# Scattering the second half's rows to the experts: a copied, looped form against a written-out form paced by TensorE's tiles

## The chip, the cores and the metric

One core of a Trainium2 chip runs the whole program. The metric is the device time of that core in microseconds (us), smaller is better. The kernel is written by hand: every engine (PE = TensorE, DVE = VectorE, ACT = ScalarE, POOL = GpSimd, SP = SyncE) has its own instruction list, and semaphores order them.

## What is computed

The reference, cut to what matters here. 64 batches of 128 tokens with 128 features pass four layers:

```python
x = x + tanh(g_xattn[0]) * _L0_xattn_ref(_layernorm(x), ctx_1024, ...)   # attention over 77 context rows
x = x + tanh(g_ffn[0])   * _L0_ffn_ref(_layernorm(x), Wg, bg, bias, W1, b1, W2, b2)
x = x + tanh(g_xattn[1]) * _L1_xattn_ref(_layernorm(x), ctx_1024, ...)
x = x + tanh(g_ffn[1])   * _L1_ffn_ref(_layernorm(x), kernel, ...)

def _L0_ffn_ref(x, Wg, bg, bias, W1, b1, W2, b2):      # mixture of 16 experts, the best 2 for each token
    logits = einsum('sbd,de->sbe', x, Wg) + bg + bias
    vals, idx = top_k(logits, 2)
    w = softmax(vals - max(vals)); cw = einsum('sbk,sbke->sbe', w, one_hot(idx, 16))
    h = relu(einsum('sbd,edh->esbh', x, W1) + b1)      # 128 -> 256
    y = einsum('esbh,ehd->esbd', h, W2) + b2           # 256 -> 128
    return einsum('esbd,sbe->sbd', y, cw)
```

The kernel computes each expert only for the tokens that chose it. For that the tokens' rows are sorted by expert through a buffer in DRAM.

## The kernel before

**Stages.** Stage A (0 to about 465 us in the trace) is the first attention layer and the expert choice, one batch per step. Stage B (about 480 to 704 us) is the experts. Stage C (from about 704 us) gathers each token's two results and does the second attention layer and the last layer.

**Halves.** The 64 batches are routed in two halves of CB = 32. When a half's logits are there, `route(c)` computes for each token two slot numbers, `POS[0]` and `POS[1]` (128 partitions x 64 batches, int32). Half 0 is routed in the middle of stage A (ROUTE0 = 40 steps), half 1 after the end of stage A. The expert input rows of all batches are kept in SBUF in `XN` (128 x 64 x 128, float32, written at L544).

**Scatters.** POOL writes each batch's 128 rows twice, once for each of the two chosen experts, to the DRAM buffer `xs_dram[c]` (the trace calls it moe_rows), with an indirect DMA of 64 KB each. The helper `scatter(c, b, p)`, L508 to L519, does one batch: it waits until the DMAs of two batches ago have landed (the semaphore `scat_made{p}`, p the parity, counts 16 for each DMA), copies the batch's row tile from `XN` to a small buffer `scat[p]` (L512), copies two columns of slot numbers to `si` (L514, two instructions), waits for these three copies (L515), and issues the two indirect DMAs (L518). Half 0's scatters lie between POOL's steps of stage A. Half 1's stand behind stage A on POOL, in a loop of 16 turns with two batches each, L564 to L566, with register addresses.

**Experts.** Each half has NT = 80 tiles of 128 rows, so stage B has 160 tiles. SP loads the tiles in groups of four (20 groups a half): `load_group`, L421 to L426, waits until TensorE has transposed all but one of the groups loaded before (`xsT_mm` counts tiles whose first transpose, L1318, is done), then issues a 256 KB load into one of two buffers `xsb`. `store_group`, L428 to L433, stores four finished tiles (L432), three groups behind the load. In front of the first load of each half, SP waits in `scattered(c)`, L415 to L419, for all 64 scatter DMAs of that half. SP's list is in order: load, store, load, store; while it waits in `scattered(1)` it stores nothing either. TensorE does per tile one transpose (L1318), one matrix product into 256 columns, two transposes (L1304) and two products, with tile t's parts spread over six steps so that the neighbours overlap. DVE adds the biases (L1053, L1046), ACT copies and applies relu (L656, L719).

**After the scatters** POOL waits for all of them to land, makes a few constants of stage C (L573 to L588), waits for half 0's stored results (L642) and issues the first gathers (L595), which read the slot numbers straight from `POS[k][:, b:b + 1]`.

The functions that the change touches:

Of the kernel before, what the change touches and what calls it, by code (L numbers as in the profile page):

```python
# [52 lines left out]
def wait_free(engine, sem, value):  # L53

    if isinstance(value, int) and value <= 0:
        return
    engine.wait_ge(sem, value)  # L57
# [31 lines left out]
def flamingo_two_layers(nc, a, out, xs_dram, ys_dram):  # L89
    NB, N, D = a["x"].shape  # L90
# [8 lines left out]
    CB = NB // NCH  # L99
# [27 lines left out]
    with ctx:  # L127
        def sb(name, shape, dt=F32):
            return ctx.enter_context(nc.sbuf_tensor(name, shape, dt))

        def sem(name):
            return ctx.enter_context(nc.semaphore(name))
# [3 lines left out]
        XN = sb("moe_in", [P, NB, D])  # L136
# [6 lines left out]
        POS = [sb(f"slot{k}", [P, NB], I32) for k in range(2)]  # L143
# [155 lines left out]
        s = {n: sem(n) for n in names}  # L299
# [3 lines left out]
        xs_flat = [xs_dram[c] for c in range(NCH)]  # L303
# [8 lines left out]
        def apart(engine):  # L312

            engine.nop(nofuse=True)  # L315
# [156 lines left out]
        def _(pool):  # L472
            g = nc.gpsimd
# [34 lines left out]
            def scatter(c, b, p):  # L508

                bb = b + c * CB  # L510
                wait_free(pool, s[f"scat_made{p}"], (bb - p) * 16)
                g.tensor_copy(scat[p], XN[:, bass.ds(bb, 1), :].rearrange("q o d -> q (o d)")).then_inc(s["idx_made"], 1)  # L512
                for k in range(2):
                    g.tensor_copy(si[2 * p + k], POS[k][:, bass.ds(bb, 1)]).then_inc(s["idx_made"], 1)  # L514
                pool.wait_ge(s["idx_made"], bb * 3 + 3)  # L515
                apart(pool)
                for k in range(2):
                    g.indirect_dma_start(out=xs_flat[c][:, :], out_offset=bass.IndirectOffsetOnAxis(ap=si[2 * p + k], axis=0),  # L518
                                         in_=scat[p], in_offset=None).then_inc(s[f"scat_made{p}"], 16)  # L519
# [41 lines left out]
            pool.wait_ge(s["ro_done"], 2)  # L561
            pool.wait_ge(s["xs_zeroed1"], 16 * CB)
            pool.wait_ge(s["XN_kept"], NB)
            with pool.Fori(0, CB // 2) as turn:  # L564
                for p in range(2):
                    scatter(1, turn * 2 + p, p)  # L566

            pool.wait_ge(s["w1_loaded"], 16 * len(loads1))
            pool.wait_ge(s["kq_step"], SETUP_STEPS)
# [4 lines left out]
            for q in range(GH):  # L574
# [3 lines left out]
                                in_=one_hot[strip, :].rearrange("q (h k) -> q h k", h=GH), compare_op=ALU.not_equal, fill=1.0,  # L578
                                base=0, pattern=[[-1, GH], [0, KW]], channel_multiplier=1).then_inc(s["c_consts"], 1)
                pool.wait_ge(s["c_consts"], 4 + 5 * q + 1)  # L580
                for c in range(NKB):
                    h, k = divmod(GH * c + q, NKB)
# [870 lines left out]
```

## Time and profile before

| | us |
|---|---|
| three timed runs | 1169.97, 1174.06, 1175.59 |
| median | 1174.06 |
| the profiled execution | 1175.44 |
| its span, first to last instruction | 1173.7 |
| PE busy in the span | 1038.0 (88%) |
| DVE, ACT, POOL busy | 821.1, 586.3, 648.8 |

The page of the profile has the busy time of each engine, the span cut into 40 slices of 29.3 us, the DMA queues, the chain that ended last, and the costliest groups of instructions. In the timelines, a row is: start in us from the span's start, duration in us, engine, line and operation, output<-inputs, how many of them in sequence (xN), and in brackets how long the engine had been idle and what ended that. "SPq" is SP's queue, which issues the DMAs of loads and stores. "PEclk" is the granted clock of TensorE as a share of 2.4 GHz; 0.5 is 1.2 GHz.

### The profile page before, as it was taken

How to read it: one execution, taken by the hardware profiler on the slowest of the kernel's cores; microseconds unless marked ns; L12 is line 12 of the kernel's file. 1: busy time of each engine (PE TensorE's matmuls, PEld its weight loads, DVE VectorE, ACT ScalarE, POOL GpSimd, SP SyncE). 2: the span in 40 equal slices, each digit the busy share in tenths (PEclk: the TensorE clock that was granted, in tenths of full speed). 3: DMA queues.
4: the chain of work that ended last, by engine and by line, in shares of the span. 5: the costliest groups of instructions: out<-in, count | busy, mean ns of one | idle time of the engine just before them, and what ended most of it. 6: DMA issues, size and time to landing. Idle time of an engine off the chain costs nothing. (4 is left out here: it accounts for less than half of the span.)

```text
span 1173.7 us, 40437 instructions
## 1 busy us (share of the span) xinstructions
PE 1038.0 (88%) x13498; PEld 847.5 (72%) x13498; DVE 821.1 (70%) x2572; ACT 586.3 (50%) x1415; POOL 648.8 (55%) x1155
## 2 busy tenths in 40 slices
PE   4999999987999995699859996899999999998893
PEld 4788887865777774488758984677777777776672
DVE  1777777776777775655525555778888888887784
ACT  2666666653566662244425552345545545454464
POOL 2333333323777677567640005477777777777756
PEclk9999999997999997699979996999999999999997
DMA  3422113221443300244333331111111111111101
GB/s 74 88 49 46 38 45 75 72 68 45 106 105 89 90 19 29 84 137 145 107 92 112 109 91 48 32 30 37 44 40 43 44 40 43 43 41 41 39 24 31
DMA packets 106902, 74.39 MB, mean 63 GB/s; under 512 B 21360, under 2 KB 98288, under 8 KB 106736
## 3 DMA queue, kind: packets, MB, share of 16 engines
q1 hardware_dynamic: 98544, 55.40, 18.0%
q0 software_dynamic: 8192, 16.79, 4.7%
q8 instruction: 102, 1.67, 0.6%
q14 instruction: 64, 0.52, 0.2%
HBM read 38.60 MB, written 33.55 MB: 61 GB/s over the span
## 5 line engine op out<-in xcount | busy, mean ns | idle before, releaser
L656 ACT ACTIVATE arena<-PS 77x512 f32<-77x512 f32 (+4 forms) x736 | 304.9, 441 | 454.9 <-PE PS L1172 265.5
L1172 PE MATMUL PS<-arena 128*32 128x128 f32 (+5 forms) x9488 | 452.6, 291 | 49.9 <-issue 16.7
L1172 PEld LDWEIGHTS PS<-arena 128*32 128x32 f32 (+4 forms) x9488 | 352.0, 145 | 129.7 <-issue 37.1
L1172 PE MATMUL PS<-w,arena 128*128 x960 | 191.7, 318 | 1.2 <-ACT arena L656 0.4
L518 POOL DMA_INDIRECT moe_rows<-arena x128 | 127.4, 996 | 71.8 <-POOL arena L514 49.5
L533 POOL TENSOR_TENSOR arena<-arena,minus_half 128x2 f32<-128x2 f32 (+1 forms) x70 | 47.5, 679 | 188.3 <-DVE arena L830 166.6
L595 POOL DMA_INDIRECT arena<-moe_results,slot x128 | 128.7, 1005 | 40.7 <-issue 31.6
L1172 PEld LDWEIGHTS PS<-w,arena 128*128 128x128 f32 x960 | 135.5, 195 | 17.0 <-issue 4.5
L637 POOL TENSOR_TENSOR arena<-arena,minus_half 128x2 f32<-128x2 f32 (+1 forms) x71 | 51.1, 720 | 172.7 <-DVE arena L1151 168.9
L1053 DVE TENSOR_TENSOR arena<-PS,b_rows 128x256 f32<-128x256 f32 x160 | 67.8, 424 | 79.0 <-PE PS L1172 65.5
L1172 PEld LDWEIGHTS PS<-arena,wk_wq 128*128 128x128 f32 x512 | 80.6, 198 | 45.6 <-issue 43.0
L1172 PE MATMUL PS<-wo,arena 128*128 128x128 f32 x640 | 100.0, 288 | 2.2 <-ACT arena L656 1.4
L1172 PE MATMUL PS<-arena,wk_wq 128*128 128x154 f32 x512 | 98.3, 317 | 1.5 <-ACT arena L656 0.8
L1065 DVE TENSOR_REDUCE arena<-PS 128x8 f32<-128x616 f32 x128 | 96.0, 791 | 3.3 <-PE PS L1172 3.2
L719 ACT ACTIVATE arena<-PS 128x256 f32<-128x256 f32 x160 | 61.4, 384 | 72.7 <-PE PS L1304 66.9
L1172 PEld LDWEIGHTS PS<-wo,arena 128*128 128x128 f32 x640 | 83.9, 193 | 13.6 <-ACT arena L656 3.4
L744 ACT ACTIVATE arena<-PS 128x1536 f32<-128x1536 f32 x64 | 93.3, 1457 | 0.0
L540 POOL TENSOR_TENSOR arena<-arena 128x616 f32<-128x616 f32 x64 | 78.1, 1220 | 21.6 <-DVE arena L896 21.5
L867 DVE TENSOR_REDUCE arena<-PS 128x8 f32<-128x616 f32 x64 | 51.2, 800 | 54.2 <-PE PS L1172 54.2
L1046 DVE TENSOR_TENSOR arena<-PS,b_rows 128x128 f32<-128x128 f32 x160 | 46.1, 288 | 34.3 <-PE PS L1172 31.3
L1249 PE MATMUL PS<-ident,arena 128*77 128x128 f32 x512 | 68.8, 277 | 1.1 <-ACT arena L656 0.9
L1126 DVE RECIPROCAL arena<-PS 128x128 f32<-128x128 f32 x64 | 61.1, 954 | 12.3 <-PE PS L1172 8.8
(149 smaller groups left out, 1656.5 us busy)
## 6 DMA issues: line engine op xcount, KB each, us to landing
moe_rows<-zeros SPq DMA_DIRECT2D x64, 160.0 KB, 2.5
arena<-moe_rows SPq DMA_DIRECT2D x40, 256.0 KB
moe_results<-arena SPq DMA_DIRECT2D x40, 256.0 KB
residual<-in_x SPq DMA_DIRECT2D x64, 64.0 KB
w<-in_W SPq DMA_DIRECT2D x32, 128.0 KB
arena<-in_ctxC SPq DMA_DIRECT2D x64, 64.0 KB
out<-arena SPq DMA_DIRECT2D x64, 64.0 KB, 1.6
arena<-in_ctxT SPq DMA_DIRECT2D x32, 77.0 KB
```

What stands on the lines that cost most here:

```text
L518: g.indirect_dma_start(out=xs_flat[c][:, :], out_offset=bass.IndirectOffsetOnAxis(ap=si[2 * p + k], axis=0), in_=scat[p], in_offset=None). ...
L540: g.tensor_tensor(pv, pv, rd0[t.par(3)].rearrange("q (h o) -> q h o", o=1).to_broadcast([P, H0, J]), ALU.mult).then_inc(s["P0_made"], 1)
L595: g.indirect_dma_start(out=gy[k][p], out_offset=None, in_=ys_flat[c][:, :], in_offset=bass.IndirectOffsetOnAxis(ap=POS[k][:, b:b + 1], axi ...
L656: A.activation(o, i, ACT.Copy).then_inc(s[done], 1)
L719: A.activation(hT[p], PS[:, 4 + p, 0:EH], ACT.Relu).then_inc(s["hT_cp"], 1)
L744: A.activation(PT1[t.par(6)].rearrange("q (g w) -> q g w", g=NG), PS[:, 4:4 + NG, 0:TAIL], ACT.Exp, scale=DH1 ** -0.5).then_inc(s["exp1"], 1)
L867: V.tensor_reduce(mx0.rearrange("q (k h) -> q k h", k=2), sv, X, ALU.max).then_inc(s["mx0_made"], 1)
L1053: V.tensor_tensor(hb[p], PS[:, 2 + p, 0:EH], b1s[:, bass.ds(e, 1), :].rearrange("q o h -> q (o h)"), ALU.add).then_inc(s["h_made"], 1)
L1065: V.tensor_reduce(mx1[:, 2 * i * KEYS:2 * (i + 1) * KEYS].rearrange("q (g k) -> q g k", g=2)[:, :, 0:GH], PS[:, 2 * i:2 * i + 2, 0:GH * J] ...
L1126: V.reciprocal(rd1, PS[:, 1, 0:P]).then_inc(s["rd1_made"], 1)
L1172: return T.matmul(o, l, r, start=start, stop=stop)
L1249: last = T.transpose(PS[0:J, 2 + h // HB0, (h % HB0) * P:(h % HB0 + 1) * P], P0[p][:, h * J:(h + 1) * J], ident[:, :])
```

## The change

Half 1's loop over `scatter(1, ...)` is replaced by 32 batches written out at build time.

- The row tile isn't copied: the DMA's source is `XN[:, b, :]`.
- The slot numbers aren't copied: the DMA's index list is `POS[k][:, b:b + 1]`.
- The wait for the three copies is gone with them. The wait for the landing of the DMAs of two batches ago stands, with a constant.
- New: batch number n of the half (n = b - 32) waits until TensorE has transposed 2n tiles (`xsT_mm`), so batch 31 waits for 62 tiles of the 80 of half 0.

Half 0's scatters are left as they are.

```diff
             pool.wait_ge(s["XN_kept"], NB)
-            with pool.Fori(0, CB // 2) as turn:
-                for p in range(2):
-                    scatter(1, turn * 2 + p, p)
+            for b in range(CB, NB):
+
+                p = b % 2
+                pool.wait_ge(s[f"scat_made{p}"], (b - p) * 16)
+                wait_free(pool, s["xsT_mm"], 2 * (b - CB))
+                apart(pool)
+                for k in range(2):
+                    g.indirect_dma_start(out=xs_flat[1][:, :],
+                                         out_offset=bass.IndirectOffsetOnAxis(ap=POS[k][:, b:b + 1], axis=0),
+                                         in_=XN[:, b, :], in_offset=None).then_inc(s[f"scat_made{p}"], 16)
```

`apart` is an empty instruction that carries a wait of its own; `wait_free` leaves out a wait for zero or less.

## Rows read from the trace of the kernel before

**Rows 1.** The page: PE's busy tenths and granted clock in 40 slices.

```profile
PE   4999999987999995699859996899999999998893
PEclk9999999997999997699979996999999999999997
```

**Rows 2.** Waits of SP's DMA queue, 480 to 700 us: total, times, longest.

```profile
SPq L57 <- DMA moe_rows<-arena: 20.0, 1, 20.0
```

**Rows 3.** Timeline of SP around the change of halves.

```profile
573.00 0.38 SPq L425 DMA_DIRECT2D arena<-moe_rows  x1
575.45 0.39 SPq L432 DMA_DIRECT2D moe_results<-arena  x1
596.28 0.37 SPq L425 DMA_DIRECT2D arena<-moe_rows  x1
```

**Rows 4.** Timeline of POOL: half 1's first instruction, one batch's period, the end.

```profile
478.82 0.29 POOL L512 COPY arena<-moe_in 128x128 f32 x1 [5.41 <-DVE tile_experts L992]
...
587.75 0.30 POOL L512 COPY arena<-moe_in 128x128 f32 x1
587.99 0.30 POOL L514 COPY arena<-slot 128x1 int32 x2
589.07 0.98 POOL L518 DMA_INDIRECT moe_rows<-arena  x1 [0.78 <-POOL arena L514]
590.35 0.96 POOL L518 DMA_INDIRECT moe_rows<-arena  x1 [0.30 <-issue]
591.31 0.30 POOL L512 COPY arena<-moe_in 128x128 f32 x1
...
593.91 0.96 POOL L518 DMA_INDIRECT moe_rows<-arena  x1 [0.30 <-issue]
596.28 1.15 POOL L573 MEMSET arena<- 128x384 f32 x4 [1.42 <-DMA moe_rows<-arena]
```

**Rows 5.** Timeline of PE: last tile of half 0, first five of half 1.

```profile
582.56 0.27 PE L1318 MATMUL PS<-ident,arena 128*128 128x128 f32 x1
...
598.97 0.48 PE L1318 MATMUL PS<-ident,arena 128*128 128x128 f32 x1 [15.04 <-DMA arena<-moe_rows]
...
606.54 0.27 PE L1318 MATMUL PS<-ident,arena 128*128 128x128 f32 x1
```

**Rows 6.** Windows, L1318 on PE alone: stretch, length, busy (count), clock, DMA share, GB/s.

```profile
489.00:583.00 94.00, 20.17 (x74) 1.00 0.44 132
606.00:699.00 93.00, 20.71 (x76) 1.00 0.37 109
480.00:561.00 81.00, 17.63 (x62) 0.95 0.42 129
```

**Rows 7.** Timeline of PE: two neighbouring tiles at full clock, and the 62nd tile.

```profile
489.24 0.27 PE L1318 MATMUL PS<-ident,arena 128*128 128x128 f32 x1
...
490.45 0.27 PE L1318 MATMUL PS<-ident,arena 128*128 128x128 f32 x1
...
559.88 0.27 PE L1318 MATMUL PS<-ident,arena 128*128 128x128 f32 x1
```

**Rows 8.** Windows, all engines: length, PE PEld DVE ACT POOL busy (count), clock, DMA share, GB/s.

```profile
500.00:575.00 75.00, 74.25 (x530) 65.70 (x529) 38.81 (x118) 35.84 (x118) 50.40 (x105) 1.00 0.46 139
620.00:690.00 70.00, 70.00 (x523) 64.27 (x522) 39.52 (x116) 38.17 (x117) 0.00 (x0) 1.00 0.37 111
760.00:860.00 100.00, 91.99 (x2048) 74.58 (x2049) 83.34 (x262) 48.81 (x125) 74.74 (x127) 1.00 0.13 37
```

**Rows 9.** Waits, all engines, 500 to 578 us: total, times, longest.

```profile
DVE arena L1053 <- issue: 8.0, 16, 0.8
```

**Rows 10.** Waits, all engines, 620 to 690 us.

```profile
DVE arena L1046 <- issue: 0.3, 1, 0.3
```

**Rows 11.** Timeline of POOL: stage C's first gathers, inside stage B.

```profile
611.16 1.01 POOL L595 DMA_INDIRECT arena<-moe_results,slot  x1 [9.03 <-DMA moe_results<-arena]
612.49 0.95 POOL L595 DMA_INDIRECT arena<-moe_results,slot  x1 [0.30 <-issue]
613.74 0.94 POOL L595 DMA_INDIRECT arena<-moe_results,slot  x1 [0.30 <-issue]
614.99 0.94 POOL L595 DMA_INDIRECT arena<-moe_results,slot  x1 [0.30 <-issue]
```

**Rows 12.** Timeline, all engines, 470 to 474 us: half 0's last scatter.

```profile
471.89 0.69 DVE L970 TENSOR_TENSOR arena<-arena 128x512 f32<-128x512 f32 x1
471.94 1.47 POOL L518 DMA_INDIRECT moe_rows<-arena  x1 [0.30 <-issue]
```

## The prediction, made blind

> **What bounds the kernel now.** I read the page's 40 slices first. PE is busy nearly all the time, and it has dips. One is in the slice from 587 to 616 us, where PE's digit and the granted clock both fall [rows 1]. That is the middle of stage B, where the work per tile is always the same, so a dip there is a wait. PE's timeline names it: the last tile of half 0 begins at 582.56 us, the first of half 1 at 598.97 us, and PE was idle for 15.04 us until a load from moe_rows landed [rows 5]. So I asked what SP was doing. Its queue waited once for 20.0 us for scatters to land [rows 2]: the store at 575.45 is its last instruction before the load at 596.28 [rows 3]. That load is released together with POOL's constants, at 596.28, by the landing of the last scatter, which POOL had begun at 593.91 [rows 4]. So between 578 and 599 us the chain is POOL scatters, landing, load, PE. Before and after, PE itself sets the pace of stage B: between 620 and 690 us it is busy 70.00 of 70 us [rows 8], and two neighbouring tiles stand 490.45 - 489.24 = 1.21 us apart [rows 7].
>
> The reader is to see that two streams run in parallel from about 480 us. PE needs its 80 tiles of half 0, POOL its 32 batches of scatters for half 1, and POOL ends later. The change speeds up POOL. What it can bring is the time that PE stands still or slow, and no more.
>
> **What is removed from POOL.** One batch now takes 591.31 - 587.75 = 3.56 us [rows 4]. Of this, 589.07 - 587.75 = 1.32 us pass from the first copy to the first DMA: the copies, then 0.78 us until the DMA starts, in which it waits for them. The rest is the two DMAs, 0.98 + 0.30 + 0.96 us. From 478.82 to the end of the last scatter at 593.91 + 0.96 = 594.87, this makes 116 us for 32 batches, or 3.63 us each.
>
> **What is left.** The changed batch is two indirect DMAs with constant addresses, whose index list is a column of `POS`. Stage C's gathers have this very form, and four of them stand 1.33, 1.25 and 1.25 us apart [rows 11], with the waits for the landed buffers between the pairs. So a batch takes 2 x 1.25 to 1.33 + 1.25, that is 2.50 to 2.58 us. I take 2.55 us. A scatter reads its index list where a gather does and differs in the direction of the data; POOL's own part, 0.94 to 1.01 us against 0.96 to 0.98 us, is the same for both [rows 4, 11]. Alone, 32 batches would need 82 us and would end at 561 us.
>
> **The added wait.** Batch n waits for 2n tiles. Behind that wait on POOL stand only the later scatters, then the constants and the gathers; nobody but SP in `scattered(1)` and stage C waits for these. PE passes tile 6 at 489.24 and needs 1.28 us a tile from there (below), so two tiles are 2.56 us: the wait is about as fast as POOL. In the slow start the tiles hold POOL up: batch 3 needs six tiles, so it starts at about 489 us instead of 486.5. The last batch needs 62 tiles; the 62nd, counted from 480 us [rows 6], begins at 559.88 [rows 7]. If POOL goes by its own rate from 489 it reaches batch 31 at 489 + 28 x 2.55 = 560.4. Both give the same: the last scatter begins at about 561.7, ends at 563 and has landed at 564, with the landing priced as now at 596.28 - 593.91 = 2.4 us from its start [rows 4].
>
> The wait for the DMAs of two batches ago costs nothing: their landing takes 2.4 us, and the newer of these DMAs was begun about 3.8 us before.
>
> **What SP does then.** It reaches `scattered(1)` at 575.8 as now, since it follows PE's tiles, and finds the wait fulfilled for 11 us. The load of group 20 has the usual wait for tile 76, at about 578. It is issued then, and PE goes on to tile 80 without a break: loads take 598.97 - 596.28 = 2.7 us to reach PE at the change of halves [rows 3, 5], and the last load of half 0, issued at 573.00 for tile 76, has more than 5 us in hand, four tiles and what the queue is ahead. The stores of groups 17 to 19 no longer stand behind the wait.
>
> **The sum.**
> - The gap: 598.97 - 582.56 = 16.41 us between tiles 79 and 80 becomes 1.21 us. That gives 15.2 us.
> - The slow clock after it: the four tiles from 598.97 to 606.54 take 7.57 us [rows 5] where four at full clock take 4.84 us. TensorE's granted clock was at the lower level, 1.2 GHz, after the idle stretch. With no idle stretch this falls away: 2.7 us.
> - Tiles 84 to 159 are 76 tiles in the window from 606 to 699 [rows 6], and I leave their time as it is.
> - Half 0's tiles: 74 of them start from 489.24 to 582.56 [rows 5 to 7]. That is 93.32 us for 73 steps, 1.278 us each, where 1.21 us would give 88.3. So 5.0 us are lost in small stalls beside the scatters. The stalls have their mark on the other engines: DVE waited 8.0 us for nothing but issue between 500 and 578 us [rows 9], and only 0.3 us between 620 and 690 us, where POOL does nothing [rows 8, 10]. The trace doesn't say whether the scatter DMAs or POOL's copies and its loop do it. If it is the copies or the loop, all 5.0 us go. If it is the DMAs and they hurt by their density, they rise: the same 64 DMAs in 84 us instead of 116. I bound it by twice the present amount, 5.0 us of loss. I take the present rate per tile, for as long as scatters run. They end 16 steps of the 73 earlier, which gives 5.0 x 16 / 73 = 1.1 us.
> - POOL's constants, now from 596.28 on [rows 4], and the first gathers, now from 611.16 on [rows 11], come 20 to 30 us earlier. They lie beside PE's tiles in both kernels, and PE waits for neither. Stage C starts when stage B ends, so it is moved as a whole, and no wait in it has a fixed time. It shows a clock of 1.00 with PE busy for 92 of 100 us [rows 8], so a longer unbroken PE stretch has no price in this trace.
>
> Together 15.2 + 2.7 + 1.1 = 19.0 us. The profiled execution took 1175.4 us, 1.4 us above the median of the timed runs, and would take 1156.4. From the median, 1174.06 - 19.0 = 1155.1 us. That is my forecast, 1.6% faster.
>
> **Rivals.**
> - *The stalls beside the scatters.* Not a different case but the two ends of a term. Gone entirely: 17.9 + 5.0 = 22.9 us, 1151.2. Doubled: 17.9 - 5.0 = 12.9 us, 1161.2. For the second speaks that the DMA engines' share rises from 0.37 without to 0.46 with scatters [rows 8]; against it, that PE lost only 5% even so.
> - *POOL gets no faster.* POOL's part of a scatter isn't always 0.97 us: half 0's last one took 1.47 us while DVE ran tensor operations of 128x512 with both inputs in SBUF [rows 12]. If reading `POS` and `XN` in place, or DVE beside it, made each that long, a batch would be 2 x (1.47 + 0.30) = 3.54 us, the scatters would end at 479 + 113 = 592 and PE would gain 2.6 us: 1171.5. Against it: DVE's operations in stage B read PSUM, and the scatters beside them took 0.98 and 0.96 us [rows 4]; they stay the same. 4%. [...]
> - *Slower: the scatters crowd out SP's loads.* Place: `load_group` in half 0, beside POOL's denser scatters, 64 DMAs in 84 us. A load has at present about 5.8 us from its issue (573.00, for tile 76 at about 578.8). From there on every further microsecond stops PE once a group. Beside about 17 groups, the gain of 17.9 us is used up when each load is late by 1.1 us, so from a landing time of 6.9 us on the kernel is slower; at 8.0 us it loses 2.2 x 17 = 37 us and stands at 1193. Against it: a load takes 2.7 us, and PE in half 0 never waited for one. 3%.
> - *The gap closes but part of the gain is lost later,* in a new order at the start of stage C or a clock that falls again: 8 to 12 us gained, 1162 to 1166. No row speaks for it. 7%.
>
> **How the numbers follow.** The forecast with its stalls between both bounds: 86%. Partly lost: 7%. POOL no faster: 4%. Slower: 3%. What a measurement of this kernel can tell from no change is about 0.5%, 5.9 us. So faster 0.93, same 0.04, slower 0.03. The range takes the stall term from its good end to its bad end, 1151.2 to 1161.2, and 2 us below for the scatter of the median (the three runs span 5.6 us): 1149.5 to 1161.5.
>
> **What would show each step.** The batch period on POOL should be 2.5 to 2.6 us with no copies, and the last scatter should end near 563 us. SP should have no wait of more than a few us for moe_rows. PE's gap of 15.04 us should be gone and the clock at full level through stage B. Tile 159 should begin near 679.5 us instead of 698.5, and stage C should have its old length. A batch period over 3 us, a PE wait on a load in half 0, or a time per tile in half 0 above 1.35 us would prove the prediction wrong.

## The result, and where the time went

The changed kernel takes 1177.1 us (median of 20 runs), the kernel before 1174.05 us (20 runs): a ratio of 1.0029, with a 95% interval of 1.0020 to 1.0038. It is slower by 3 us, where I had forecast 19 us less.

The gap that the change was to close is closed. PE's timeline in the changed kernel, at its tiles 79 and 80 (the same two tiles as in [rows 5]; L1325 here is L1318 there):

```profile
603.14 0.27 PE L1325 MATMUL PS<-ident,arena 128*128 128x128 f32 x1
...
604.35 0.27 PE L1325 MATMUL PS<-ident,arena 128*128 128x128 f32 x1
```

They stand 1.21 us apart, and the list of waits of SP's queue has no entry for moe_rows any more, where it had 20.0 us [rows 2]. But tile 79 comes at 603.14 instead of 582.56. The gain at the change of halves was lost ahead of it. Windows of the changed kernel, all engines (columns as in [rows 8]):

```profile
485.00:583.00 98.00, 84.13 (x527) 70.52 (x527) 38.63 (x115) 35.14 (x117) 54.92 (x58) 0.93 0.37 112
604.00:700.00 96.00, 94.61 (x702) 86.36 (x702) 52.77 (x157) 51.19 (x156) 3.86 (x4) 1.00 0.37 108
```

In half 0 PE is busy for 84 of 98 us, its clock falls below full for short stretches (0.93 in the mean), and DVE and ACT do over a quarter fewer operations a microsecond than beside half 1. The account, tile by tile: from tile 6 (488.31) to tile 79 (603.14) 114.8 us pass, where it was 93.3, a loss of 21.5 us. The gap gives 15.2 and the slow clock behind it 2.7 us. Tile 6 comes 0.9 us earlier, half 1 takes 97.4 us for the 96.8 of the forecast. Together tile 159 begins at 701.76 instead of 698.53; from there to the end it is 474.0 us against 475.2.

What slows half 0? Not a load: PE has no wait for a load between 488 and 583 us. POOL's timeline shows how the scatters go now:

```profile
541.91 0.96 POOL L571 DMA_INDIRECT moe_rows<-moe_in,slot  x1 [1.81 <-PE PS L1325]
543.17 0.95 POOL L571 DMA_INDIRECT moe_rows<-moe_in,slot  x1 [0.30 <-PE PS L1325]
544.43 0.96 POOL L571 DMA_INDIRECT moe_rows<-moe_in,slot  x1 [0.30 <-issue]
545.69 0.95 POOL L571 DMA_INDIRECT moe_rows<-moe_in,slot  x1 [0.30 <-issue]
548.48 0.95 POOL L571 DMA_INDIRECT moe_rows<-moe_in,slot  x1 [1.83 <-PE PS L1325]
```

The pairs of [rows 4] have become longer runs, 1.26 us from start to start, with the pause that the tile wait makes between the runs. POOL stood idle for over 1.3 us 16 times between the 64 scatters, which makes 17 runs: eleven of four, the others of two to six. ACT in the same stretch, and PE's transposes that it waits for:

```profile
543.18 0.28 ACT L663 ACTIVATE arena<-PS 128x128 f32<-128x128 f32 x1 [0.16 <-PE PS L1325]
544.71 0.38 ACT L726 ACTIVATE arena<-PS 128x256 f32<-128x256 f32 x1 [1.25 <-PE PS L1311]
546.17 0.28 ACT L663 ACTIVATE arena<-PS 128x128 f32<-128x128 f32 x1 [1.07 <-PE PS L1325]
547.67 0.38 ACT L726 ACTIVATE arena<-PS 128x256 f32<-128x256 f32 x1 [1.23 <-PE PS L1311]
547.95 0.27 ACT L663 ACTIVATE arena<-PS 128x128 f32<-128x128 f32 x1
```

```profile
544.08 0.27 PE L1325 MATMUL PS<-ident,arena 128*128 128x128 f32 x1
...
545.29 0.27 PE L1325 MATMUL PS<-ident,arena 128*128 128x128 f32 x1
```

The reader is to compare the ends. The transpose of 544.08 is over at 544.35, ACT is free at 545.09, and yet its copy begins at 546.17. Its input is done and it is free, and it starts 1.1 us late. The operation itself takes the usual 0.28 us. DVE is late in the same stretch, and both are back in time at 547.7, 2.0 us after the start of the last scatter of the run. Then the next run starts and it begins again.

From the DMA packets in the trace one more number is needed: a scatter's last packet ends 1.9 us after the scatter's start on POOL where nothing disturbs it. So the next scatter, 1.26 us behind it, is begun while this one is under way.

### The profile page after: what moved, and what is told of

The parts are those of the page before. It is cut to its first block and busy times, and to the rows that moved or that the text cites. A ratio compares the mean times of both kernels' runs of the same rounds, so it can differ in the third digit from the quotient of the medians.

```text
span 1175.8 us, 40164 instructions
## 1 busy us (share of the span) xinstructions
PE 1040.9 (89%) x13498; PEld 847.2 (72%) x13498; DVE 820.6 (70%) x2572; ACT 586.6 (50%) x1415; POOL 631.0 (54%) x1059
## 5 line engine op out<-in xcount | busy, mean ns | idle before, releaser
L1179 PE MATMUL PS<-w,arena 128*128 x960 | 194.2, 321 | 10.9 <-issue 4.9
L751 ACT ACTIVATE arena<-PS 128x1536 f32<-128x1536 f32 x64 | 93.3, 1457 | 0.0
L571 POOL DMA_INDIRECT moe_rows<-moe_in,slot x64 | 61.2, 957 | 51.0 <-issue 28.9
L518 POOL DMA_INDIRECT moe_rows<-arena x64 | 65.5, 1023 | 35.2 <-POOL arena L514 25.4
```

Source lines behind the costliest of these rows:

```text
L571: g.indirect_dma_start(out=xs_flat[1][:, :], out_offset=bass.IndirectOffsetOnAxis(ap=POS[k][:, b:b + 1], axis=0), in_=XN[:, b, :], in_offs ...
L751: A.activation(PT1[t.par(6)].rearrange("q (g w) -> q g w", g=NG), PS[:, 4:4 + NG, 0:TAIL], ACT.Exp, scale=DH1 ** -0.5).then_inc(s["exp1"], 1)
L1179: return T.matmul(o, l, r, start=start, stop=stop)
```

## The experiments

**The theories.** Theory 1: the late stretches come from scatters in unbroken runs, each begun before the one ahead has landed. Theory 2: the tile wait is at fault, POOL waiting on the counter that TensorE raises. Theory 3: reading rows and slot numbers in place. Theory 1 got its present words after e1 to e4; e5 to e12 were forecast with them. Two more came up then: 4, the mean rate of scatters alone; 5, only starts right behind each other.

Each kernel differs from the changed one in half 1's scatters on POOL alone.

### e1: no tile wait

```diff
                 pool.wait_ge(s[f"scat_made{p}"], (b - p) * 16)
-                wait_free(pool, s["xsT_mm"], 2 * (b - CB))
```

> The changed kernel without the wait for TensorE's tiles; the rest of the change stands. Theory 1 (runs of scatters): ACT and DVE answer late from the landing of the first scatter of an unbroken run to the landing of its last. Without the tile wait all 64 scatters form one run of 82 us (479 to 561 us), so TensorE's tiles stay slow all that time, 1.6 to 2.3 us each, then 1.21 us: 1172 to 1185 us in all, and the last scatter starts near 560. Theory 2 (the tile wait itself holds POOL and TensorE in step and costs the time): the gap is closed and nothing is slow, 1155 us. Theory 3 (reading the rows and slot numbers in place slows the other engines): as the changed kernel, about 1177 us, 1.57 us a tile.

Measured: 1227.6 us, ratio 1.0448 (1.0431 to 1.0466). Scatters go at 2.53 us a batch, as the forecast had it, and the last starts at 561.04. But stage B nearly stands still meanwhile. ACT's timeline, and PE's transposes (L1309) that its first row waits for:

```profile
520.09 0.38 ACT L724 ACTIVATE arena<-PS 128x256 f32<-128x256 f32 x1 [15.12 <-remote]
529.19 0.28 ACT L661 ACTIVATE arena<-PS 128x128 f32<-128x128 f32 x1 [8.72 <-remote]
```

```profile
491.21 0.38 PE L1309 MATMUL PS<-ident,arena 128*128 128x128 f32 x2
```

ACT had its input from 491.59 us on and was idle from 504.97, and started at 520.09. The semaphore that these transposes raise is recorded at 520.07. PE began two tiles between 495 and 555 us, where full speed gives 49; its clock was 0.52 in the mean there, which explains a factor of two and not of twenty. Theory 2 is out: without the tile wait it is much worse. Theory 1 has the right sign, but I had expected 1.6 to 2.3 us a tile and it was 14 (70.4 us for five tiles, up to the last scatter). The tile wait was not the cost but a brake: it broke the run whenever TensorE fell behind.

### e2: the copies put back, tile wait kept

```diff
+                g.tensor_copy(scat[p], XN[:, b, :]).then_inc(s["idx_made"], 1)
+                for k in range(2):
+                    g.tensor_copy(si[2 * p + k], POS[k][:, b:b + 1]).then_inc(s["idx_made"], 1)
+                pool.wait_ge(s["idx_made"], b * 3 + 3)
+                apart(pool)
...                 (the scatters read si and scat[p])
```

> Written out and with the tile wait, but with the three copies and the wait for them put back. Theory 1: the copies part the scatters into pairs with a pause of 1.3 us, a batch takes 3.4 to 3.56 us, the tile wait is always fulfilled; as the kernel before, 1170 to 1175 us, 1.28 us a tile in half 0, PE idle for 12 to 15 us at the change of halves. Theory 2: the tile wait is there, so over 1176 us. Theory 3: as the kernel before.

Measured: ratio 0.9990 (0.9981 to 1.0000), 47 tiles begun from 495 to 555 us, 47 in the kernel before. Written out and with the tile wait, at this pace, the kernel is as before, as theories 1 and 3 had it.

### e3, e9, e10, e11, e4: pairs with a pause

No tile wait; rows and slot numbers in place; behind each pair of scatters a memset into a buffer of its own, which nothing reads.

```diff
-                wait_free(pool, s["xsT_mm"], 2 * (b - CB))
...
+                pause(b - CB, W)     # W columns: 480, 640, 780, 920, 1070
...
+            def pause(n, w):
+                wait_free(pool, s["idx_made"], 3 * CB + n)
+                g.memset(pad[:, 0:w], 0.0).then_inc(s["idx_made"], 1)
```

> The changed kernel without the tile wait, and with a memset of 480 columns (about 0.5 us, into a buffer that nothing reads) behind each pair of scatters. A batch takes 3.0 to 3.1 us, the last scatter starts near 576 us. Theory 1: pairs again, so the stalls are as short as before, 1.28 to 1.32 us a tile, and the gap at the change of halves shrinks to 0 to 2 us: 1157 to 1163 us. Theory 2: 1155 to 1160 us. Theory 3: stalls as in the changed kernel, 1.5 us a tile or more, 1175 us or more.

> As e3, with a memset of 1070 columns (about 1.0 us), so that a batch takes 3.5 to 3.6 us as before the change, with rows and slot numbers read in place. Theory 1 and theory 2: as the kernel before, 1171 to 1175 us, 1.28 us a tile in half 0. Theory 3: 1.4 us a tile or more, and over 1176 us.

> As e3 and e4 (no tile wait, a memset behind each pair), the memset of 640 columns: the next pair starts 1.77 us after the second scatter of a pair. The landing takes 1.89 us, so the run is never broken. Theory 1: nearer to e3 (1199 us) than to e4 (1168 us): 1185 to 1199 us. If the loss only went with the mean rate of scatters, a line from e3 (1.64 us, 1199) to e4 (2.13 us, 1168) would give 1191 us.

> The memset of 780 columns: 1.89 us from the second scatter of a pair to the next pair, the very time of a landing. Theory 1: the edge; some runs are broken and some not, 1165 to 1185 us.

> The memset of 920 columns: 2.0 us from the second scatter of a pair to the next pair, a batch in 3.27 us. Theory 1: undisturbed landings of 1.89 us end before the next pair begins, so 1.27 to 1.30 us a tile as in e4, and the last scatter starts 4 us earlier than there: 1163 to 1167 us, faster than both kernels and than e4.

| kernel | from the pair's second scatter to the next pair, us | last scatter starts | tiles begun, 495 to 555 us | ratio to the kernel before |
|---|---|---|---|---|
| e1 (no pause) | 1.26 | 561.0 | 2 | 1.0448 (1.0431 to 1.0466) |
| e3, 480 columns | 1.64 | 573.2 | 21 | 1.0207 (1.0190 to 1.0224) |
| e9, 640 | 1.77 | 575.6 | 28 | 1.0101 (1.0068 to 1.0134) |
| e10, 780 | 1.89 | 581.3 | 41 | 0.9954 (0.9932 to 0.9977) |
| e11, 920 | 2.0 | 584.1 | 48 | 0.9920 (0.9895 to 0.9946) |
| e4, 1070 | 2.13 | 587.2 | 47 | 0.9940 (0.9924 to 0.9957) |
| before (copies) | 2.27 | 593.9 | 47 | 1 |

Less than half a microsecond more pause, from e3 to e11, turns the slowest of the paused kernels into the fastest. The turn lies where theory 1 puts it, near the 1.9 us of a landing: below that the next pair begins while the last scatter is under way. I had read e3 wrongly beforehand: I took pairs for pairs, whatever the pause, and forecast 1157 to 1163 us. e4 also does away with theory 3. It reads everything in place and is faster than the kernel before (and 2.7 us below its forecast), by what its shorter batch gives: PE idles 7.60 us at the change of halves instead of 15.04 us.

e11 beats the kernel before by 0.8% and, by the two ratios, the changed one by 1.1%. Its POOL timeline:

```profile
542.68 0.97 POOL L576 DMA_INDIRECT moe_rows<-moe_in,slot  x1 [0.16 <-issue]
543.95 0.96 POOL L576 DMA_INDIRECT moe_rows<-moe_in,slot  x1 [0.30 <-issue]
544.92 0.88 POOL L569 MEMSET pause<- 128x920 f32 x1
545.96 0.97 POOL L576 DMA_INDIRECT moe_rows<-moe_in,slot  x1 [0.17 <-issue]
```

And PE's first tile of half 1 in it:

```profile
589.53 0.47 PE L1331 MATMUL PS<-ident,arena 128*128 128x128 f32 x1 [5.51 <-DMA arena<-moe_rows]
```

A third of the old gap is left, with half 0 at its old speed. e11's lead over e4 isn't settled. They ran on different chips, each beside the kernel before (1179.4 and 1174.7 us there), and in the profiled executions e10 and e11 took 4 and 6 us longer than e4 from tile 159 to the end, which these kernels leave alone; e12, which ran on e11's chip, took 5 us longer there too. The intervals of the ratios overlap.

### e12: e4 with the tile wait

```diff
                 pool.wait_ge(s[f"scat_made{p}"], (b - p) * 16)
+                wait_free(pool, s["xsT_mm"], 2 * (b - CB))
...
                 pause(b - CB, 1070)
```

> e4 (pairs, memset of 1070 columns) with the tile wait of the change put back. Theory 1: at 3.4 us a batch the tiles are always ahead of the wait, so it does nothing: as e4, 0.994 of the kernel before, 1.27 us a tile. Theory 2 (POOL waiting on the counter that TensorE raises slows the others): over 1176 us.

Measured: 0.9945 (0.9924 to 0.9966), 48 tiles. As e4. The tile wait does nothing where it is always fulfilled.

### e8: runs of four

```diff
-                pool.wait_ge(s[f"scat_made{p}"], (b - p) * 16)
-                wait_free(pool, s["xsT_mm"], 2 * (b - CB))
+                if b % 2 == 0:
+                    for q in range(2):
+                        pool.wait_ge(s[f"scat_made{q}"], b * 16)
```

> As e6, but two batches (four scatters) go in one run and the next run waits for the landing of all four. The mean time of a batch is (3 x 1.26 + 1.9 + 0.2) / 2 = 2.95 us, the rate of e3, where the queue was never empty. Theory 1: late stretches of 3.9 us in every 5.9 us; a tile takes about 1.6 us while scatters run, the last scatter starts near 573 us; between the changed kernel and e3, 1172 to 1185 us. Theory 4: as e3, 1199 us.

Measured: 1.0049 (1.0034 to 1.0064), 36 tiles begun from 495 to 555 us, the very number of the changed kernel. Its late stretches repeat every 6.8 us and are 3.7 us long, from 2.2 us after a run's first scatter to 2.1 us after its last, and while scatters run it makes 1.6 us a tile, as forecast. It took 6.8 us and not 5.9 for two batches, since POOL goes on later after a landing than I had priced:

```profile
509.16 0.96 POOL L571 DMA_INDIRECT moe_rows<-moe_in,slot  x1 [0.30 <-DMA moe_rows<-moe_in,slot]
512.14 0.96 POOL L571 DMA_INDIRECT moe_rows<-moe_in,slot  x1 [2.02 <-issue]
```

That makes it a cleaner test of theory 4 than planned. From first to last scatter it takes 108.1 us (478.32 to 586.39), e4 takes 108.3 (478.89 to 587.2). The mean rate is the same; in pairs it leaves 47 tiles, in fours 36. It is the length of the run that counts, not the rate. And it has no tile wait: the changed kernel's loss doesn't need it, only its runs.

### e6 and e7: waiting for the landing

```diff
# e6
-                pool.wait_ge(s[f"scat_made{p}"], (b - p) * 16)
-                wait_free(pool, s["xsT_mm"], 2 * (b - CB))
+                for q in range(2):
+                    pool.wait_ge(s[f"scat_made{q}"], (b + 1 - q) // 2 * 32)
...
# e7, before each scatter (the same two lines removed)
+                    for q in range(2):
+                        pool.wait_ge(s[f"scat_made{q}"], (b + 1 - q) // 2 * 32 + (16 * k if q == p else 0))
```

e6 waits before each pair for the landing of all earlier scatters, e7 before each single one.

> Rows and slot numbers read in place, no tile wait, no pause; instead each batch waits until both scatters of the batch before have landed. Theory 1, now sharper (the other engines answer late whenever a scatter is begun before the one ahead has landed, until one lands with none behind it): only the second scatter of each pair is such a one, so the late stretches are 1.2 us long as in the kernel before, 1.27 us a tile in half 0. A batch takes 1.26 + 1.9 + 0.2 = 3.3 to 3.4 us, the last scatter starts near 584 us, PE idles 5 to 8 us at the change of halves: 1164 to 1168 us. Theory 4 (what counts is the mean rate of scatters, at any spacing): between e3 and e4, 1175 us or more.

> As e6, but every single scatter waits for the landing of the one before it. Theory 1: no scatter is begun behind one under way, so ACT and DVE have no late stretch at all and half 0 goes at 1.21 us a tile (tile 79 near 577 us). A scatter takes 1.9 + 0.2 us, the last starts near 610 us, so PE idles for over 30 us and the whole takes 1184 to 1192 us. Theory 4: the mean rate falls by a tenth against the kernel before, so the stalls stay, 1.27 us a tile.

Measured: e6 1.0289 (1.0275 to 1.0303), e7 1.0762 (1.0746 to 1.0779). As forecasts of the time both were wrong, in the price of the wait. In e7 POOL's starts are at best 2.98 us apart:

```profile
516.06 0.96 POOL L570 DMA_INDIRECT moe_rows<-moe_in,slot  x1 [2.02 <-DMA moe_rows<-moe_in,slot]
519.04 0.96 POOL L570 DMA_INDIRECT moe_rows<-moe_in,slot  x1 [2.02 <-issue]
```

A scatter whose last packet ends 1.9 us after its start lets POOL begin the next at 2.98, not at 2.1. Its semaphore is raised at 2.05 to 2.22 us, so about 0.75 us of this lie on POOL behind the landing. In e6 it was often later still: from the second scatter of a pair to the next pair 3.05 us in the median and 3.4 in the mean. So the last scatters start at 623.8 and 682.2 us, and PE waits 52 us for the load in e6.

On the mechanism they were right. In half 0 of e7 all 501 records of a raised semaphore of stage B come within 0.02 us of the operation's end; none is late. Windows on PE's first transpose alone, 495 to 555 us, of the kernel before, e6, e7 and e8 in this order (columns as in [rows 6]):

```profile
495.00:555.00 60.00, 12.80 (x47) 1.00 0.48 143
```

```profile
495.00:555.00 60.00, 13.36 (x49) 1.00 0.45 136
```

```profile
495.00:555.00 60.00, 13.64 (x50) 1.00 0.42 126
```

```profile
495.00:555.00 60.00, 9.76 (x36) 1.00 0.38 115
```

With single scatters half 0 runs at 1.209 us a tile, that is without any loss, the only one of these kernels that does.

### e5: evenly spaced scatters

```diff
-                wait_free(pool, s["xsT_mm"], 2 * (b - CB))
...
+                    pause(2 * (b - CB) + k, 180)      # behind each scatter, about 0.25 us
```

> No tile wait, and a memset of 180 columns (about 0.25 us) behind each scatter, so that scatters start evenly, some 1.5 us apart, with no runs, at the mean rate of e3. A scatter lands 1.9 us after its start, so at 1.5 us each begins before the one ahead has landed, without a break. Theory 1: late all the time, as in e1 or e3, 1200 us or more. Theory 5 (only starts right behind each other, 1.26 us apart, do it): as the kernel before or better in half 0, the gap nearly closed, 1160 us.

Measured: 1.0410 (1.0394 to 1.0426), 8 tiles from 495 to 555 us. The starts came 1.39 us apart, evenly, never right behind each other, and always under the 1.9 us of a landing. Theory 5 is out. (A batch took 2.78 us and not the 3.0 planned, so it is no clean test of theory 4; e8 is.)

## Why the prediction was wrong

**Right:** the views named the bound. POOL's copies cost 1 us a batch, and without anything in its way POOL makes 2.53 us a batch (e1). The gap of 15.2 us and the slow clock's 2.7 us went. Tile 80 follows tile 79 in 1.21 us. Half 1 takes what it took. Nothing in stage C gave the time back.

**Wrong:** one term of the sum, the stalls beside the scatters. I saw 5.0 us of them in the kernel before, forecast 1.1 us less, and bounded the bad end at twice the amount, 5.0 us of loss. It was 21.5 us of loss, and half 0 took 1.57 us a tile, over the 1.35 that I had named as a sign of being wrong. The step that failed is the sentence "the same 64 DMAs in 84 us instead of 116. I bound it by twice the present amount". It took the stalls for something that goes by number or by density, smoothly. They go by the length of a run. In a pair the second scatter makes ACT and DVE late for about 1.2 us, and that costs little: 5.0 us in all. I take it that the pipeline of six steps over which a tile is spread soaks up most of it; no run varies the pipeline. In a run of four it is 3.7 to 4 us, which e8 and the changed kernel pay for in tiles, and in a run of 49 (e1) nearly everything stops.

With that the second error follows: the last scatter at 563 us. Since PE slowed down, and the tile wait tied POOL to PE, it was 583.73. The two streams that I had priced one by one were coupled both ways.

**It could have been read in the trace of before.** The price of a run of four stands there. The gathers of [rows 11] are four indirect DMAs 1.25 to 1.33 us apart, from 611.16 to 615.93, beside tiles of half 1. PE's transposes right there, in the kernel before:

```profile
615.00 0.27 PE L1318 MATMUL PS<-ident,arena 128*128 128x128 f32 x1
...
616.93 0.27 PE L1318 MATMUL PS<-ident,arena 128*128 128x128 f32 x1
...
618.74 0.27 PE L1318 MATMUL PS<-ident,arena 128*128 128x128 f32 x1
```

Two tiles in 3.74 us instead of 2.42: one run of four costs 1.32 us. 64 scatters in runs of four would cost 16 x 1.32 = 21 us, where the kernel before loses 5.0. With this term the sum would have been 17.9 - 16 = 2 us gained, 1172 us. That is still short of the measured loss: against 1.21 us a tile the changed kernel loses 26.5 us and e8, whose scatters do go in fours, 27.7, that is 1.7 us a run. And that the runs are mostly of four, and not without end, is the work of the tile wait, which I had priced as costing nothing. I took the period of the scatters from these gathers and didn't look at what stood beside them. That the two steps from tile 91 to tile 93 are the only ones of half 1 so long, once the clock is full again, would have been the hint. ACT's lateness was to be seen too. In the kernel before, during the second scatter of a pair (549.09):

```profile
549.42 0.27 PE L1318 MATMUL PS<-ident,arena 128*128 128x128 f32 x1
...
550.66 0.28 ACT L656 ACTIVATE arena<-PS 128x128 f32<-128x128 f32 x1 [1.09 <-PE PS L1318]
```

The transpose ends at 549.69, ACT starts at 550.66, and the semaphore is recorded as raised at 550.64. A lag of a microsecond between a releaser's end and the start of an idle engine was the warning.

The mark that I took for the stalls was the wrong one. DVE's 8.0 us of "issue" [rows 9] have their like in e7, 6.3 us in 13 waits in the same window, and e7 loses nothing. They go with the scatters and not with lost time.

**The rivals.** "Slower: the scatters crowd out SP's loads" had the sign and the neighbourhood, and the wrong mechanism: by their packets the loads of half 0 still landed within 2.0 to 3.8 us, at least 2.8 us ahead of their tiles. "POOL gets no faster" is not what happened, nor did DVE hold up POOL: each scatter took 0.96 us of it, none over 0.97.

**Durations and starts.** In the kernels with runs, the operations of ACT and DVE take what they always took, 0.28, 0.38 and 0.42 us; only their starts are late. With the durations agrees the Trainium skill, "SBUF — State Buffer", § Who interferes with whom: a DMA never contends with a compute engine. That is said of SBUF's ports. It is no promise that scatters can't hold up compute engines: in e1 ACT sat idle for 15.12 us with its input there, because the semaphore came late.

**What stays open:** what it is that holds back the raising of semaphores while scatters follow on each other. ACT, DVE, PE and SP were all late, and so were the records of the scatters' own landings. Where on the way between an engine or a DMA and the semaphore they are held, and why the landing of the last scatter sets them free, no run here tells. That gathers do it as well rests on the one run of four gathers above, where the records are up to 1.8 us late and the last of them come 2.1 us after the last gather's start. It wasn't tried whether smaller scatters, landing in under 1.26 us, could follow each other freely.

## What to carry to other kernels

In this kernel an indirect DMA from POOL that starts before the one ahead has landed costs the other engines time, and the cost grows with the length of the run. So before removing work between such DMAs, look at that work as a pause: here the copies kept the runs at two. Count runs and their lengths, and space the pairs by a little more than a landing (2.0 us after the last start here) with plain work; waiting for the landing itself costs POOL another microsecond.

Where the trace of before shows the pattern that the change will make, even once and in another stage, price the change by that spot and by all engines around it, not by the duration of the one instruction.

## What the runs showed of the hardware that I had not expected

- While indirect scatters overlap, semaphores are raised late: in the changed kernel up to 3.8 us after the end of the operation that raises them, in e1 28.5 us (491.59 to 520.07), and ACT begins 0.02 us after the record. With single scatters that each wait for the landing of the one ahead none is late (e7, half 0, 501 records).
- Beside 64 indirect scatters of 64 KB, 1.26 us apart with one longer step of 2.76 us behind the 49th, ACT, DVE and PE nearly stopped: 2 tiles in 60 us where 49 are normal (e1).
- The effect sets in sharply between 1.77 and 2.0 us from the last start of a pair to the next: 28, 41 and 48 tiles in 60 us at 1.77, 1.89 and 2.0 us.
- POOL begins an indirect DMA that waits for the landing of another 2.98 us after that one's start, though the last packet ends after 1.9 us (e7).
- The Trainium skill, "DMA: Bandwidth & Descriptors", § Anatomy of one DMA — SWDGE (gpsimd) path, gives for a DMA issued by GpSimd about 2.0 us and the bytes over 436 GB/s, for 64 KB an estimate of 2.15 us. The trace agrees: in e7 the semaphore of the scatter of 513.09 is raised from 515.14 to 515.31 us, 2.05 to 2.22 us after its start. POOL's next one begins 0.75 us behind that, at 516.06.
